# Two scan rows' input products in one GpSimd instruction, in a Mamba layer with a mixture of experts

## What is computed

```python
delta = softplus(einsum('blr,dr->bld', dt_lo, dt_proj_w) + dt_proj_b)
def step(h, inp):
    d_t, B_t, C_t, x_t = inp
    dA = exp(d_t[..., None] * A)                 # 1024 channels x 16 states
    h = h * dA + d_t[..., None] * B_t[:, None, :] * x_t[..., None]
    y_t = sum(h * C_t[:, None, :], axis=-1)
    return (h, y_t)
y = (y + x * D) * silu(z)
out = einsum('bld,ed->ble', y, out_proj_w)
# then: layernorm(x + out), gate over 8 experts, top 2, expert matmuls, layernorm
```

## Time and profile before

| what | us |
|---|---|
| median of 3 timed runs | 2342.28 (2341.37 to 2342.51) |
| profiled execution, its own time | 2345.1 |
| its span in the profile | 2343.3 |
| VectorE busy | 2103.1 (90%) |
| TensorE busy | 2087.0 (89%) |
| GpSimd busy | 1802.6 (77%) |
| ScalarE busy | 1517.8 (65%) |

### The profile page before, as it was taken

How to read it: one execution, slowest core, us unless ns; L and a number is a source line. 1 busy time by engine, 2 the same in 40 slices (tenths; PEclk the granted TensorE clock), 3 DMA queues, 4 the chain that set the end, 5 groups by cost and what they waited for, 6 DMA issues and landing times.

```text
span 2343.3 us, 30148 instructions
## 1 busy us (share of the span) xinstructions
PE 2087.0 (89%) x8604; PEld 1212.1 (52%) x8604; DVE 2103.1 (90%) x2369; ACT 1517.8 (65%) x2742; POOL 1802.6 (77%) x1448
## 2 busy tenths in 40 slices
PE   8896789897989989899899998899898998879998
PEld 3444455555555555545555555445555455555543
DVE  5799999999999999899999999999998998899833
ACT  5747855785577766678567775778566875556411
POOL 2959997798887888779887888879887896686402
PEclk9897889898999999899999999999998999789999
DMA  5312041357544674346752576446743567565523
GB/s 172 109 38 71 19 141 49 119 188 257 154 110 148 208 270 126 108 153 225 261 121 104 182 270 191 108 159 201 270 126 100 172 216 253 131 227 177 190 75 81
DMA packets 205314, 367.93 MB, mean 157 GB/s; under 512 B 28472, under 2 KB 34744, under 8 KB 205152
## 3 DMA queue, kind: packets, MB, share of 16 engines
q1 hardware_dynamic: 190496, 335.60, 42.8%
q0 software_dynamic: 12544, 29.37, 5.9%
q10 hardware_dynamic: 2112, 1.05, 0.2%
HBM read 287.05 MB, written 78.91 MB: 156 GB/s over the span
## 4 chain that ended last, share of the span: by engine, by line
PE 29%; DVE 25%; POOL 25%; issue 11%; DMA 4%; ACT 4%; SPq 1%; DVEq 0%; POOLq 0%; ACTq 0%
PE bank L1040 19%; POOL dbu L1481 15%; DVE hst L1685 10%; DVE y L1515 6%; PE hTp L1054 6%; DVE hst L1693 3%; DVE u L1544 3%; POOL u L1469 3%; POOL delta L1466 2%; DMA zs<-sorted_tokens 2%; DMA ysb<-sorted_results,place 1%; POOL zs L1448 1%; POOL dbu L1489 1%; ACT dA L1386 1%; PE bank L1173 1%
## 5 line engine op out<-in xcount | busy, mean ns | idle before, releaser
L1481 POOL TENSOR_TENSOR dbu<-u,Bbc 128x512 f32<-128x512 f32 x896 | 1145.5, 1315 | 197.0 <-DVE hst L1685 190.3
L1685 DVE TENSOR_TENSOR_SCAN hst<-dA,dbu 128x512 f32<-128x512 f32 x896 | 1054.1, 1211 | 20.8 <-ACT dA L1386 15.5
L1386 ACT ACTIVATE dA<-delta,negA 128x512 f32<-128x512 f32 (+1 forms) x1152 | 723.5, 639 | 457.1 <-DVE hst L1685 364.7
L1054 PE MATMUL hTp<-ident,hst 128*128 128x128 f32 x4096 | 572.6, 292 | 130.4 <-DVE y L1515 36.4
L1054 PEld LDWEIGHTS hTp<-ident,hst 128*128 128x128 f32 x4096 | 503.5, 151 | 356.3 <-issue 145.1
L1515 DVE SCALAR_TENSOR_TENSOR y<-hTp,Ct,y 128x1024 f32<-128x1024 f32 x512 | 648.3, 1266 | 40.4 <-PE hTp L1054 39.7
L1040 PE MATMUL bank<-wslot,hidT 128*128 128x512 f32 x512 | 247.9, 619 | 19.9 <-ACT zs L1330 15.9
L1489 POOL TENSOR_TENSOR dbu<-u,Bbc 128x512 f32<-128x512 f32 x128 | 163.1, 1309 | 82.1 <-DVE hst L1693 65.8
L1040 PE MATMUL bank<-delta,tokT 128*128 128x512 f32 x480 | 223.2, 602 | 1.5 <-issue 0.8
L1040 PE MATMUL bank<-wslot,tokT 128*128 128x512 f32 x464 | 219.6, 603 | 3.1 <-ACT tokT L1345 2.5
L1040 PE MATMUL bank<-hidT,wslot 128*128 128x512 f32 x384 | 187.1, 630 | 9.8 <-DVE u L1544 7.6
(11 more groups left out here) (150 smaller groups left out, 2479.9 us busy)
## 6 DMA issues: line engine op xcount, KB each, us to landing
wslot<-in_w_expT SPq DMA_DIRECT2D x85, 1024.0 KB, 6.0
Bbc<-b_scratch SPq DMA_DIRECT2D x113, 256.0 KB, 3.5
zs<-sorted_tokens SPq DMA_DIRECT2D x105, 256.0 KB, 3.0
sorted_results<-ysb SPq DMA_DIRECT2D x105, 256.0 KB, 6.0
wslot<-in_w_inT SPq DMA_DIRECT2D x26, 1024.0 KB, 5.4
res<-in_w_expT SPq DMA_DIRECT2D x18, 1024.0 KB, 5.7
gate_scratch<-zs SPq DMA_DIRECT2D x64, 256.0 KB, 2.3
delta<-in_w_outT SPq DMA_DIRECT2D x14, 1024.0 KB, 10.5
```

What stands on the lines that cost most here:

```text
L1054: mm = nc.tensor.transpose(hTp[q % 2][:, tok(j)], hst[n % 2][:, j, start:start + P], ident[:, :])
L1386: nc.scalar.activation(decay_of(step, halved), delta[w.odd][:, j, cols], ACT.Exp, scale=negA[:, j, n:n + 1]).then_inc(exp_done, 1)
L1481: nc.gpsimd.tensor_tensor(dbu[j % 4][:, :], u[w.odd][:, j, :], Bbc[n % 2][:, :], ALU.mult).then_inc(dbu_done, 1)
L1685: nc.vector.tensor_tensor_scan(hst[n % 2][:, j, :], dA[j % 2][:, :], dbu[j % 4][:, :], 0.0, ALU.mult, ALU.add).then_inc(scan_done, 1)
```

## The change

One GpSimd instruction now makes the products of two rows, j and j+1 with j even, for all 512 tokens: it reads `u[:, j:j+2, :]` and the same row of B twice, and writes two neighbouring blocks of `dbu`, which becomes one tensor of 4 blocks in place of four tensors. It is issued at the even row; the odd row issues no multiplication, only its pieces. It waits until both blocks are free, so for the scan of row j-3 (`scan_done` at n*8 + j - 2), and in the first state of a period for `u` of both blocks. `dbu_done` counts pairs: both scans of a pair wait for the same count, and SyncE's waits on it are recounted by `products`. The halved part is as before, but for the buffer's name. Each period of the seven that are not halved has 64 such instructions in place of 128.

```diff
-        dbu = [sb(f"dbu{s}", [P, L]) for s in range(4)]
+        dbu = sb("dbu", [P, 4, L])
...
+        def products(b):
+
+            return b * (NS * ND // 2) if b < NB else (b + 1) * (NS * ND // 2)
...
-                            sync.wait_ge(dbu_done, w.b * (NS * ND) + m * (ND // 2 if w.seg.halved else ND))
+                            sync.wait_ge(dbu_done, products(w.b) + m * (ND // 2))
...
-                    if w.seg.steps and not w.seg.halved:
+                    if w.seg.steps and not w.seg.halved and j % 2 == 0:
                         if j == 0:
                             pool.wait_ge(b_loaded[n % 2], w.b * (16 * NS // 2) + 16 * (n // 2 + 1))
                         if n == 0:
-                            pool.wait_ge(u_ready, w.b * ND + (j + 1))
+                            pool.wait_ge(u_ready, w.b * ND + (j + 2))
                         if not (w.seg is SEG_PRO and n == 0 and j < 4):
-                            pool.wait_ge(scan_done, w.b * (NS * ND) + (n * ND + j - 3))
-                        nc.gpsimd.tensor_tensor(dbu[j % 4][:, :], u[w.odd][:, j, :], Bbc[n % 2][:, :], ALU.mult).then_inc(dbu_done, 1)
+                            pool.wait_ge(scan_done, w.b * (NS * ND) + (n * ND + j - 2))
+                        nc.gpsimd.tensor_tensor(dbu[:, j % 4:j % 4 + 2, :], u[w.odd][:, j:j + 2, :],
+                                                Bbc[n % 2][:, :].unsqueeze(1).broadcast_to((P, 2, L)), ALU.mult).then_inc(dbu_done, 1)
...
-                        dve.wait_ge(dbu_done, w.b * (NS * ND) + tile)
+                        dve.wait_ge(dbu_done, products(w.b) + (n * ND + j) // 2 + 1)
...
-                        nc.vector.tensor_tensor_scan(hst[n % 2][:, j, :], dA[j % 2][:, :], dbu[j % 4][:, :], 0.0, ALU.mult, ALU.add).then_inc(scan_done, 1)
+                        nc.vector.tensor_tensor_scan(hst[n % 2][:, j, :], dA[j % 2][:, :], dbu[:, j % 4, :], 0.0, ALU.mult, ALU.add).then_inc(scan_done, 1)
```

More of the change, by code:

```diff
@@ L944, in piece @@
                     elif s == 8:
-                        sync.wait_ge(dbu_done, NB * (NS * ND))
+                        sync.wait_ge(dbu_done, products(NB))
                         sync.sem_inc(seen_sp, 1)
@@ L956, in piece @@
                     elif t == PAIR:
-                        sync.wait_ge(dbu_done, w.b * (NS * ND))
+                        sync.wait_ge(dbu_done, products(w.b))
                         sync.sem_inc(seen_sp, 1)
@@ L1488, in period @@
                         pool.wait_ge(scan_done, w.b * (NS * ND) + (k - 3 if k < 4 else 2 * k - 6))
-                        nc.gpsimd.tensor_tensor(dbu[k % 4][:, :].rearrange("p (k t) -> p k t", k=2), u[w.odd][:, j:j + 2, cols],
+                        nc.gpsimd.tensor_tensor(dbu[:, k % 4, :].rearrange("p (k t) -> p k t", k=2), u[w.odd][:, j:j + 2, cols],
                                                 Bbc[n % 2][:, cols].unsqueeze(1).broadcast_to((P, 2, HL)), ALU.mult).then_inc(dbu_done, 1)
@@ L1690, in period @@
                         dve.wait_ge(exp_done, w.b * (NS * ND) + (step // 2 * 2 + 2))
-                        dve.wait_ge(dbu_done, w.b * (NS * ND) + (step // 2 + 1))
+                        dve.wait_ge(dbu_done, products(w.b) + (step // 2 + 1))
                         dve.wait_ge(hT_done, w.b * (NS * NH) + (n - 1) * (NH if n < 2 else PAIR))
-                        nc.vector.tensor_tensor_scan(hst[n % 2][:, j, start:stop], decay_of(step, True), dbu[step // 2 % 4][:, step % 2 * HL:(step % 2 + 1) * HL],
+                        nc.vector.tensor_tensor_scan(hst[n % 2][:, j, start:stop], decay_of(step, True), dbu[:, step // 2 % 4, step % 2 * HL:(step % 2 + 1) * HL],
                                                      hst[n % 2][:, j, kept:kept + 1] if c else 0.0, ALU.mult, ALU.add).then_inc(scan_done, 1)
```

## The result

| what | before | after |
|---|---|---|
| median of timed runs, us | 2342.4 (2341.37 to 2342.68, 4 runs) | 2388.24 (2382.67 to 2391.99, 4 runs) |
| profiled execution, its own time | 2345.1 | 2391.99 |
| its span | 2343.3 | 2390.2 |
| mean granted TensorE clock | 0.937 | 0.918 |

The changed kernel is slower by a factor of 1.018, with a 95% interval of 1.0153 to 1.0206: some 46 us. I had forecast 2361 and a range of 2344 to 2378. The direction was right, the time lies outside the range, and the miss (27 us) is larger than the loss that I did predict (19 us).

What follows compares the result with a forecast made beforehand. VectorE was taken to bound the kernel, with GpSimd ahead, held by the four-buffer ring. New waits 17.2 + 2 + 4.0 + 1.1 = 24.3 us, less 5 given back, leave 19: 2361 us median, range 2344 to 2378.

Steps and rivals of the forecast that it cites:

- The pair's duration: GpSimd's product of two rows: 2.40 us (2.0 to 2.55) in place of two products of 1.22 to 1.23 us spacing.
- The plain stretches cost nothing: Plain y, scan, scan cycles: 2.1 us of margin hide one piece between pairs, so no cost.
- Place 1, the tap: Scatters and sigmoid product in five middle periods: late product delays VectorE's first convolution tap, 3 x 3.8 + 2 x 2.9 = 17.2 us.
- Place 1, the second period: Second period, other order: sigmoid product at 448.2 some 3.5 us late, reaching VectorE through ScalarE's tap; 2 us.
- Places 2 and 3: First gy of a period, four places: pair 0.8 to 1.1 us late, 4.0 us; first scan at the start: 1.1 us.
- The failed step: Steady part: some of VectorE's 91.6 us idle time shrinks as TensorE catches up in stalls; 5 us given back.
- GpSimd's chain is the bound: Faster rival: GpSimd's 25% of the chain of waits sets the end, so saved work gives about 2325 us; chance 0.08.
- Absorbed: No-change rival: late sigmoid products are made good by less waiting for TensorE; 2342 to 2347 us; chance 0.14.
- Coarse grain everywhere: Slower rival: pairs of 2.6 us or more, or late GpSimd pieces, exceed the plain cycle's margin; 2385 us; chance 0.13.

Runs made afterwards that it cites:

- the two singles: Changed kernel's order and wait, but two 128x512 instructions, one behind the other at the even row, in place of the pair; 2393.26 us, ratio 1.0194.
- the wait at that row alone: Kernel before, with the later wait (scan j-3) only at row 4 of state 9 in the five middle periods; 2366.37 us, ratio 1.0085.
- the fillers: Changed kernel plus 32 useless 128x128 TensorE products ahead of its wait for the convolution in the five middle periods; 2367.61 us, ratio 1.0089.

## Why the prediction was wrong, point by point

- **The pair's duration.** Predicted 2.40 us, measured 2.394 (the estimate by the Trainium skill, GPSIMD Engine Reference, was 2.35; the measurement decides). GpSimd's wait for scans was to be over 250 us and is 333.0. Right, and the duration mattered little, as the two singles show. Of the other signs, ScalarE's wait for sigmoid products was to grow by 18 us and grew by 33 (7.7 to 40.4); VectorE's wait for taps grew by 20.
- **The plain stretches cost nothing.** Right as far as can be told: 401 pairs at rows without pieces give a ratio of 1.0017 (0.9997 to 1.0036).
- **Place 1, the tap: 17.2 us.** Right: 16.1 in the changed kernel, 17.17 with the wait at that row alone. Scatter, sigmoid product and activation came within 0.3 us of where the sum had put them.
- **Place 1, the second period: 2 us.** The wait came, with the size that I gave it, by another link, and was absorbed. ScalarE waited 4.39 us for the sigmoid product (until 459.79), its decay was late, not its tap, and VectorE's scan at 461.03 waited 2.05 us. But before, VectorE had waited 2.42 us for TensorE at 463.90, and that wait is gone: the lag grows by 2.14 and falls by 2.50.
- **Places 2 and 3: 4.0 and 1.1 us.** The start's wait grew by 1.1 (2.72 to 3.8). At the four gy places the lag grows by 0.6, 0.9, 1.75 and 0.5 us, 3.8 in all, partly given back; the direct waits for products there are only some 0.6 us (4.4 in all, 3.8 of it at the start), so the way in which it comes was not as I had it. Right in size, small in the sum.
- **The failed step** is the sentence "Some of its 91.6 us of idle time in the steady part [...] will shrink when TensorE catches up in a stall [...] I give back a fifth, 5 us." I took the stall for something that the rest of the pipeline may use to catch up. What the runs show in its place: TensorE can't use it, since it waits for the same convolution; its idle time grows from 2.09 to 5.66 us; its clock falls to 0.50; and it then takes 3.77 us for what took 1.98. The prediction had itself said, in the words left out here, that TensorE's banks are late with the same convolutions; it put the price of that at nothing and gave no reason. It cost 26.0 us (13.9 and 12.1). With the fillers, that is without the clock's fall, the time was 2367.6, 22.4 us above the 2345.2 of its series, which lies between the forecast's 19 and its 24.3 before anything is given back. That closeness is in part luck: the sum had nothing for the gathers, which cost 6.9 us there and 7.4 in the changed kernel, and too little for what is given back elsewhere.
- **The rivals.** "GpSimd's chain is the bound" falls: its share of the chain rose from 25% to 35% while its work shrank, and kernels that keep 401 pairs are no faster. A large share of the chain did not mean that the engine's work sets the time; when its instructions may start did. "Absorbed" falls with the result. "Coarse grain everywhere" named 2385, 3 us from the median, by another mechanism: it wanted 18 to 20 us of direct waits for products, and there are 4.4. The number came out by accident.

The sign of what the clock can do was to be seen in the profile before. TensorE waited up to 3.0 us for the convolution there, and the window from 1020 to 1030 us already had a granted clock of 0.83. I had read that column only as a mean, 0.937. The Trainium skill (TensorE: Matmul & The Clock Gate, Part 1) says that the clock has two levels and that the lower one follows idling of the array; every row above agrees with this. It also says that the moment of a change isn't tied to the program. That would fit the first middle period, where an idle stretch of 5.73 us left the clock at 0.89 and cost nothing more. It is not that what TensorE does behind the stall is cheaper in that period: with the two singles the clock stood at 0.50 for 14 us there and the lag grew by 2.6 us to the copy of C. What decides in a given period how long the clock stays down is open; so the 26.0 us are those of one execution, and the fillers' 20.6, a difference of medians, is the safer price.

## What to carry to other kernels

When a change lengthens an idle stretch of TensorE, price the stretch twice: once as the wait itself, and once as the work behind it at half clock, if that work is on anyone's path; how long the half clock lasts can differ from period to period (3 to 20 us here). The granted clock by stretches, not its mean, shows how near the kernel already is. Merging two instructions on an engine that is ahead of its consumer saved nothing here, and in a ring of buffers it made the release coarser: look for the pieces that stand behind the merged instruction's wait, since five such places, with what followed them, made 42.1 of 46.9 us here. A filler that does nothing is a good experiment for telling a slow clock from a late input.

## What the runs showed of the hardware that I had not expected

- After 5.66 us of idling TensorE ran at 0.50 of its clock for 20 us, from 1031 to 1050 us, though it was busy without a break from 1032 on. At that level four matmuls of 64x512 took 3.77 us in place of 1.98, and eight transposes 1.97 in place of 1.09.
- The same idling (5.73 us) at 754 us brought 0.61 over four microseconds, 0.89 over the ten from 755, and no further delay. The length of the slow stretch and the loss go together, and the idle time does not tell the length: in the run with the later wait at one row, at 5.9 us of idling, 7 us of slow clock cost nothing, 14 cost 3.0 and 20 cost 6.4.
- One GpSimd product of 128x1024 takes 2.394 us, and 2.34 by the spacing of two without a pause (786.98 to 791.66); two of 128x512 take 2.46 by their spacing. Half the instructions save 5% of the time of these products by spacing, 6.5% by GpSimd's busy time (1145.5 to 1070.7).
- 32 fp32 products of 128x128 took 7.3 us (64 records of 0.114 us each), where I had expected 4.2.
